# Attention and ternary feed-forward on one core: attention outputs stored without gaps, and Wo's product over two tiles of 128 rows

## The chip, the cores and the metric

The kernel runs on one core of a Trainium2 chip. The metric is the device time of one execution in microseconds (us), median of several runs.

## The reference

One transformer layer for a sequence of 4096 tokens of width 256, in f32:

```python
q, k, v = (x @ W.T + b, split into 16 heads of 16)      # Wq, Wk, Wv
q, k = rope(q), rope(k)
scores = softmax(q @ k.T / 16)                           # per head
x1 = layernorm(x + (scores @ v) @ Wo.T)
h = silu((x1 @ w1.T) * s1) * ((x1 @ w2.T) * s2)          # 256 -> 1024
h = gelu((h @ h1.T) * t1);  h = gelu((h @ h2.T) * t2)    # 1024 -> 1024, twice
out = layernorm(x1 + (h @ w3.T) * s3)                    # 1024 -> 256
```

The w and h matrices are ternary before a scaling of the inputs.

## The kernel before

The program has three parts, one after the other. Within a part every engine has its own instruction stream, and semaphores order them.

`project` computes q, k and v. `attend` works through 32 units: 8 chunks of 512 query tokens (CH), times 4 groups (NG) of 4 heads (HG). For one unit TensorE computes the scores of 128 keys by 512 queries, ScalarE takes their exponentials, and TensorE multiplies these with v (L547). The v tile has a 17th column of ones, so the products of one head fill 17 rows: 16 rows of output and one row of the softmax's sum. The four heads of a group lie at partitions 0, 32, 64 and 96 of the PSUM tile `sums`, so rows 17 to 31 of each stretch of 32 carry nothing of use. ScalarE copies this tile to `mixed` (L664, two buffers), and the queue of SyncE stores all 128 rows into `heads_dram` in one transfer (`finish`, L422 to L426). `attend` ends with SyncE waiting until the last stores have landed (L452 to L454).

`feed_forward` works through the 8 chunks of 512 tokens:

- `load_heads` (L847) loads one chunk as `heads_sb`, 128 partitions by 4 groups by 512, and then the chunk of x. For chunk c+2 it is issued once `front_apply` of chunk c+1 is done.
- `load_sums`, `store_inverse` and `load_shares` (L830 to L843): the sums' rows come in as 128 x 64, VectorE inverts them (`invert`, L1137), they go out to `shares_dram`, and are loaded again so that each head's row of 512 reciprocals is repeated over the head's partitions: four transfers of 64 KB for each of the four groups, into two buffers. VectorE multiplies them in (`divide`, L1148), one instruction for each group.
- `front` (L928) is Wo's product: per chunk 4 token tiles by 4 groups of 128 rows. The trace counts two matmuls for each f32 product, 32 per chunk. wo has the layout of heads_sb, with zeros in the rows without use; GpSimd sets them (L893).
- `gate_layer`, two `hidden_layer`s and `back` are the feed-forward products (L964, L1008). TensorE's order for chunk c, in `step`, is: hidden_layer 0, front(c+1), hidden_layer 1, front_flip(c+1) (L947), back(c), gate_layer(c+1).
- VectorE's `step` begins with divide(c+1, 0) and (c+1, 1), and places divides 2 and 3 behind the first two `gelu_split`s.

For chunk 0 the sums, stores and shares go through SyncE's queue, in this order: sums, heads, x, inverse, wo, scales, shares, then the large weights (L877). For later chunks GpSimd issues sums, inverse and shares, and SyncE issues the heads.

Of the kernel before, what the change touches and what calls it, by code (L numbers as in the profile page):

```python
# [328 lines left out]
def attend(nc, io, q_parts, k_parts, heads_dram, w_dram, low_bits, v_all, k_all):  # L329
# [6 lines left out]
    with ExitStack() as ctx:  # L336
# [72 lines left out]
        def _(sp):  # L409
# [42 lines left out]
            for p in range(2):  # L452
                sp.wait_ge(mixed_free[p], 16 + 16 * UNITS // 2)
            sp.wait_ge(w_copied, 16 * len(W_AT))  # L454
# [197 lines left out]
        @block.scalar  # L652
        def _(act):
            act.sem_inc(probs_free, RING // HG)

            act.wait_ge(first_turn, 1)
            act.activation(shift[:], scores[0][0:QT, 0:P], ACT.Copy, scale=-1.0).then_inc(exps_done, BANKS)

            def take_sums(c, g):

                act.wait_ge(probs_free, (c * NG + g + 1) * KT + RING // HG)

                act.wait_ge(mixed_free[g % 2], (c * 2 + g // 2) * 16 + 16)
                act.activation(mixed[g % 2][:], sums[:], ACT.Copy).then_inc(sums_free, 1)  # L664

            def unit(c, g, first=False, last=False):
                u = c * NG + g
                for n in range(TILES):
                    if n == TURN_AT and not last:
                        act.wait_ge(scored, u * SLOTS + n + 1)  # L670

                        act.wait_ge(part_step, (u + 2) * ROUNDS)
                        act.activation(shift[:], scores[n % BANKS][0:QT, 0:P], ACT.Copy, scale=-1.0)\  # L673
                            .then_inc(exps_done, 1)
                    s = slot(n, not last)
                    act.wait_ge(scored, u * SLOTS + s + 1)
                    if n % HG == 0:

                        act.wait_ge(probs_free, u * KT + n // HG + 1)
                    bank = last_banks[n % len(last_banks)] if last else scores[s % BANKS][:]  # L680
                    act.activation(probs[n % RING][:], bank, ACT.Exp, scale=INV_SCALE)\  # L681
                        .then_inc(exps_done, 1)
                    if n == HG - 1 and not first:
                        take_sums(*((c, g - 1) if g > 0 else (c - 1, NG - 1)))

            unit(0, 0, first=True)
            for c in range(NCH - 1):
                for g in range(1, NG):
                    unit(c, g)
                unit(c + 1, 0)  # L690
            for g in range(1, NG):
                unit(NCH - 1, g, last=g == NG - 1)
            take_sums(NCH - 1, NG - 1)

        @block.vector
        def _(dve):
# [25 lines left out]
            for p in range(2):  # L722
                dve.sem_inc(mixed_free[p], 16)
            dve.sem_inc(wide_free, 2)
# [13 lines left out]
def feed_forward(nc, io, heads_dram, shares_dram, w_dram, low_bits, out):  # L738
# [7 lines left out]
    with ExitStack() as ctx:  # L746
# [15 lines left out]
        flag = sb("flag", [1, 1], I32)  # L762
        heads = sb("heads_sb", [P, NG, CH])

        inverse_sums = sb("inverse_sums", [P, HG * NG * CH // P])
        shares = [sb(f"shares{b}", [P, CH]) for b in range(2)]
# [21 lines left out]
        x_in = sem("x_ff_in")  # L788
        wo_zero = sem("wo_zero")
        ident_set = sem("ident_ff_set")  # L790
# [27 lines left out]
        HIDS = 3 * HT  # L818
        SUM_COLS = HG * NG * CH // P
        SUM_ROWS = P // HG  # L820
        NORM1 = 4 * TT + 2
        NORM2 = 5 * TT + 2
        SMALL = HG + 4 + 1
        EARLY = 3
# [5 lines left out]
        def load_sums(engine, c, done):  # L830

            for j in range(HG):
                src = heads_dram[bass.ds(c, 1), 32 * j + HD].rearrange("c g (a b) -> (c g a) b", b=SUM_COLS)
                engine.dma_start(inverse_sums[j * SUM_ROWS:(j + 1) * SUM_ROWS], src).then_inc(done, 16)

        def store_inverse(engine, c, done):
            dst = shares_dram[bass.ds(c, 1)].rearrange("c j g (a b) -> (c j g a) b", b=SUM_COLS)
            engine.dma_start(dst, inverse_sums[:]).then_inc(done, 16)

        def load_shares(engine, c, g, done):  # L840
            for j in range(HG):
                src = shares_dram[bass.ds(c, 1), j, g].rearrange("c s -> (c s)").partition_broadcast(32)
                engine.dma_start(shares[g % 2][32 * j:32 * j + 32], src).then_inc(done[g % 2], 16)  # L843

        @block.sync
        def _(sp):
            def load_heads(c):  # L847
                sp.dma_start(heads[:], heads_dram[bass.ds(c, 1)].rearrange("c p g s -> (c p) g s")).then_inc(heads_in, 16)
                sp.dma_start(x_sb[:], io["x"].rearrange("(c t p) d -> c p t d", t=TT, p=P)[bass.ds(c, 1)]
# [20 lines left out]
            sp.wait_ge(first_inverse_out, 16)  # L870
            for g in range(NG):
                if g >= 2:

                    sp.wait_ge(divided, g - 1)
                load_shares(sp, 0, g, first_shares_in)

# [15 lines left out]
        def _(pool):  # L892
            pool.memset(wo[:], 0.0).then_inc(wo_zero, 1)  # L893
            pool.wait_ge(wo_zero, 1)
            pool.memset(ones[:], 1.0).then_inc(ident_set, 1)
# [8 lines left out]
            with pool.Fori(1, NCH) as c:  # L904
# [22 lines left out]
        def _(pe):  # L927
            def front(c):  # L928


                pe.wait_ge(divided, c * NG + NG)
                for t in range(TT):
                    if t % 2 == 0 and not (isinstance(c, int) and c == 0):

                        pe.wait_ge(norm2, (c - 1) * NORM2 + t + 2)
                    for g in range(NG):
# [173 lines left out]
        def _(dve):  # L1110
# [20 lines left out]
            def invert(c):  # L1131

                if isinstance(c, int) and c == 0:
                    dve.wait_ge(first_sums_in, HG * 16)
                else:
                    dve.wait_ge(sums_in, c * HG * 16)
                dve.reciprocal(inverse_sums[:], inverse_sums[:]).then_inc(inverted, 1)  # L1137

            def divide(c, g):

                if g == 0:
                    dve.wait_ge(heads_in, c * 16 + 16)

                if isinstance(c, int) and c == 0:
                    dve.wait_ge(first_shares_in[g % 2], (g // 2 + 1) * HG * 16)
                else:
                    dve.wait_ge(shares_in[g % 2], ((c - 1) * 2 + g // 2 + 1) * HG * 16)
                dve.tensor_tensor(heads[:, g], heads[:, g], shares[g % 2][:], ALU.mult).then_inc(divided, 1)  # L1148

# [85 lines left out]
            invert(0)  # L1235
            for g in range(NG):
                divide(0, g)
            dve.wait_ge(small_in, 16 * SMALL)
# [62 lines left out]
```

## Time and profile before

| | |
|---|---|
| time, median of 3 runs | 3553.01 us (3552.21 to 3554.25) |
| the profiled execution | 3551.05 us, of it 3549.4 us from its first to its last instruction (the span) |
| TensorE busy | 3414.3 us, 96% |
| VectorE busy | 2997.2 us, 84% |
| ScalarE busy | 2451.1 us, 69% |
| `attend` ends, `feed_forward` begins | at about 2785 us of the span |
| granted TensorE clock, mean | 0.971 |

A matmul's busy time overlaps that of its neighbours, so the duration of a stretch of them is read from the chain or from start to start.

### The profile page before, as it was taken

What the parts mean: (1) busy time and instruction counts of PE and PEld (TensorE: products, weight loads), DVE (VectorE), ACT (ScalarE), POOL (GpSimd) and SP (SyncE); (2) the same over time, 40 slices, a digit from 0 to 9 for tenths busy, and PEclk for the clock granted to TensorE, in tenths of its full rate; (3) what the DMA queues carried; (4) which work ended last, traced back from release to release, by engine and by line L of the source; (5) the groups of instructions that cost most, each with busy time, mean ns of one, the idle gap of its engine ahead of it and who ended that gap; (6) DMA issues with size and microseconds to landing.
All of it is one profiled execution on the core that took longest, in us unless ns stands there. A gap on an engine that the chain in (4) does not pass through costs nothing. (4 is left out here: it accounts for less than half of the span.)

```text
span 3549.4 us, 67886 instructions
## 1 busy us (share of the span) xinstructions
PE 3414.3 (96%) x28122; PEld 1560.8 (44%) x28122; DVE 2997.2 (84%) x3204; ACT 2451.1 (69%) x4472; POOL 242.7 (7%) x440
## 2 busy tenths in 40 slices
PE   8569999999999999999999999999999699999998
PEld 3223333333333333333333333333333388888887
DVE  6599999999999999999999999999994245555554
ACT  2108888888888888888888888888889422222222
POOL 3300000000000000000000000000000011111100
PEclk8759999999999999999999999999999799999999
DMA  8920000000000010001000000000000501111100
GB/s 211 222 36 12 16 14 14 25 13 13 14 30 18 12 62 13 14 13 61 18 17 25 15 14 14 14 14 13 17 8 5 187 31 37 37 37 37 37 19 13
DMA packets 64150, 126.12 MB, mean 36 GB/s; under 512 B 13447, under 2 KB 25800, under 8 KB 62648
## 3 DMA queue, kind: packets, MB, share of 16 engines
q1 hardware_dynamic: 54920, 102.49, 10.3%
q0 software_dynamic: 8928, 19.35, 1.9%
q8 instruction: 221, 3.62, 0.4%
q14 instruction: 81, 0.66, 0.1%
HBM read 90.59 MB, written 41.16 MB: 37 GB/s over the span
## 5 line engine op out<-in xcount | busy, mean ns | idle before, releaser
L710 DVE TENSOR_REDUCE group_max<-wide 128x2 f32<-128x1024 f32 x2048 | 2473.0, 1222 | 23.9 <-PE wide L521 17.2
L681 ACT ACTIVATE probs<-scores 128x512 f32<-128x512 f32 x4046 | 2202.9, 600 | 291.8 <-PE scores L606 43.9
L547 PE MATMUL sums<-probs,v_all 128*17 128x256 f32 (+1 forms) x16120 | 1277.9, 389 | 7.7 <-ACT mixed L664 6.8
L606 PE MATMUL scores<-q_sb,k_all 51*128 51x512 f32 x3968 | 989.0, 495 | 6.7 <-ACT probs L681 5.7
L521 PE MATMUL wide<-k_all,q_sb 48*128 48x512 f32 x4096 | 850.6, 411 | 52.4 <-DVE group_max L710 26.7
L606 PEld LDWEIGHTS scores<-q_sb,k_all 51*128 51x128 f32 x3968 | 370.9, 183 | 843.5 <-ACT probs L681 830.0
L547 PEld LDWEIGHTS sums<-probs,v_all 128*17 128x17 f32 x16120 | 267.1, 95 | 748.1 <-issue 365.8
L521 PEld LDWEIGHTS wide<-k_all,q_sb 48*128 48x128 f32 x4096 | 397.8, 191 | 91.0 <-DVE group_max L710 63.9
L1083 ACT ACTIVATE whole_hid<-acc,scale 128x512 f32<-128x512 f32 x128 | 84.7, 689 | 321.7 <-PE acc L964 316.9
L964 PE MATMUL acc<-hid_b,h2T 128*128 128x512 f32 x1024 | 241.6, 396 | 0.0
L964 PE MATMUL acc<-hid_a,h1T 128*128 128x512 f32 x1024 | 240.2, 394 | 0.0
L964 PEld LDWEIGHTS acc<-hid_b,h2T 128*128 128x128 f32 x1024 | 192.3, 188 | 46.4
L964 PEld LDWEIGHTS acc<-hid_a,h1T 128*128 128x128 f32 x1024 | 191.6, 187 | 47.3
L1173 DVE CAST hid_a<-whole_hid 128x512 fp32r<-128x512 f32 x128 | 54.4, 425 | 185.7 <-ACT whole_hid L1083 183.5
L1074 ACT ACTIVATE gate<-acc,scale 128x512 f32<-128x512 f32 x64 | 44.1, 690 | 125.9 <-PE acc L964 125.9
L229 PE MATMUL ps_qk<-xt,w_qk 128*128 128x512 f32 x128 | 72.6, 729 | 27.7 <-DMA xt<-in_xT 27.6
L1175 DVE TENSOR_TENSOR hid_a<-whole_hid,hid_a 128x512 fp32r<-128x512 f32 x128 | 88.6, 692 | 4.4
L1182 DVE SCALAR_TENSOR_TENSOR whole_hid<-acc,scale,gate 128x512 f32<-128x512 f32 x64 | 48.1, 751 | 44.9 <-PE acc L964 44.9
L937 PE MATMUL tok<-wo,heads_sb 128*128 128x256 f32 x256 | 59.3, 392 | 17.8 <-DVE heads_sb L1148 17.8
L964 PE MATMUL acc<-x1t,w1T 128*128 128x512 f32 x256 | 71.8, 402 | 2.1 <-DVE x1t L1167 2.1
L1173 DVE CAST hid_b<-whole_hid 128x512 fp32r<-128x512 f32 x64 | 27.1, 424 | 55.1 <-ACT whole_hid L1083 55.0
L483 POOL CAST shift_parts<-shift 16x128 bf16<-16x128 f32 x32 | 8.9, 279 | 932.7 <-ACT shift L673 896.7
(89 smaller groups left out, 1295.0 us busy)
## 6 DMA issues: line engine op xcount, KB each, us to landing
k_all<-k_parts SPq DMA_DIRECT2D x96, 128.0 KB, 5.1
q_sb<-q_parts SPq DMA_DIRECT2D x192, 64.0 KB, 2.8
q_parts<-parts SPq DMA_DIRECT2D x16, 512.0 KB, 5.9
k_parts<-parts SPq DMA_DIRECT2D x16, 512.0 KB, 6.3
heads<-mixed SPq DMA_DIRECT2D x32, 256.0 KB, 2.6
heads_sb<-heads SPq DMA_DIRECT2D x8, 1024.0 KB, 4.9
shares<-shares_dram POOLq DMA_DIRECT2D x112, 64.0 KB, 2.3
xt<-in_xT SPq DMA_DIRECT2D x8, 512.0 KB, 6.3
```

The lines of the kernel that those rows point to most:

```text
L229: last = pe.matmul(ps[m][:], w_sb[:, t, i, ft * P:(ft + 1) * P], xt[p][:, i], start=(i == 0), stop=(i == FT - 1))
L521: last = pe.matmul(wide[n % 2][:, e], q_sb[g][rows, j, t * P:(t + 1) * P], k_all[rows, g * GP + j, b * CH:(b + 1) * CH], start=True, stop= ...
L547: last = pe.matmul(sums[32 * j:32 * j + HD + 1, cols], v_all[:, g, kt, j], probs[(kt * HG + j) % RING][:, cols], start=(kt == 0 and cols.s ...
L606: pe.matmul(scores[(s + e) % BANKS][:], k_all[rows, g * GP + j, n // HG * P:(n // HG + 1) * P], q_sb[g][rows, j], start=True, stop=True).t ...
L681: act.activation(probs[n % RING][:], bank, ACT.Exp, scale=INV_SCALE)\
L710: dve.reduce_max(group_max[:, n], wide[n % 2][:], AX_X).then_inc(wide_free, 1)
L937: last = pe.matmul(tok[t // 2][:, t % 2], heads[:, g, t * P:(t + 1) * P], wo[:, g], start=(g == 0), stop=(g == NG - 1))
L964: mm = pe.matmul(dst, w.bitcast(view), src[h].bitcast(view), start=(first and h == 0), stop=(last and h == 1))
L1083: act.activation(whole[o % 4][:], acc[n % 4][:], ACT.Gelu, scale=scale[:, 2 + layer, o:o + 1])\
L1173: dve.tensor_copy(dst[0][:, k % HT], whole[k % 4][:]).then_inc(rounded, 1)
L1175: dve.tensor_tensor(dst[1][:, k % HT], whole[k % 4][:], dst[0][:, k % HT].bitcast(F32), ALU.subtract)\
L1182: dve.scalar_tensor_tensor(out=whole[o % 4][:], in0=acc[(2 * o + 1) % 4][:], scalar=scale[:, 1, o:o + 1], in1=gate[o % 2][:], op0=ALU.mult ...
```

## The change

Heads lie in DRAM as 16 heads by 17 rows, without gaps. `finish` stores four pieces of 17 rows in place of one of 128. `load_heads` loads the 16 output rows of eight heads as one tile of 128 rows, twice. The sums come in by one transfer in place of four. The shares of a chunk are spread by two transfers, whose source has the dimensions 8 heads, 16 repeats, 512, in place of sixteen. `divide` runs twice per chunk, and `front` has 4 token tiles by 2 tiles of 128 rows, 8 products (16 matmuls in the trace's count). wo loads in one transfer, and GpSimd's memset of it is gone. `mixed_free` counts four transfers for each store.

```diff
@@ attend
             def finish(c, g):
                 sp.wait_ge(sums_free, c * NG + g + 2)
-                sp.dma_start(heads_dram[bass.ds(c, 1), :, g].rearrange("c p s -> (c p) s"), mixed[g % 2][:])\
-                    .then_inc(mixed_free[g % 2], 16)
+                for j in range(HG):
+                    sp.dma_start(heads_dram[c, g * HG + j], mixed[g % 2][32 * j:32 * j + HD + 1]).then_inc(mixed_free[g % 2], 16)
@@ feed_forward
-        wo = sb("wo", [P, NG, D])
+        wo = sb("wo", [P, FT, D])
-        heads = sb("heads_sb", [P, NG, CH])
+        heads = sb("heads_sb", [P, FT, CH])
         def load_sums(engine, c, done):
-            for j in range(HG):
-                src = heads_dram[bass.ds(c, 1), 32 * j + HD].rearrange("c g (a b) -> (c g a) b", b=SUM_COLS)
-                engine.dma_start(inverse_sums[j * SUM_ROWS:(j + 1) * SUM_ROWS], src).then_inc(done, 16)
+            src = heads_dram[bass.ds(c, 1), :, HD].rearrange("c h (a b) -> (c h) a b", b=SUM_COLS)
+            engine.dma_start(inverse_sums[:], src).then_inc(done, 16)
-        def load_shares(engine, c, g, done):
-            for j in range(HG):
-                src = shares_dram[bass.ds(c, 1), j, g].rearrange("c s -> (c s)").partition_broadcast(32)
-                engine.dma_start(shares[g % 2][32 * j:32 * j + 32], src).then_inc(done[g % 2], 16)
+        def load_shares(engine, c, f, done):
+            src = shares_dram[bass.ds(c, 1), f * HF:(f + 1) * HF].rearrange("c h s -> (c h) s")
+            engine.dma_start(shares[f][:], src.unsqueeze(1).to_broadcast([HF, HD, CH]))\
+                .then_inc(done[f], 16)
             def load_heads(c):
-                sp.dma_start(heads[:], heads_dram[bass.ds(c, 1)].rearrange("c p g s -> (c p) g s")).then_inc(heads_in, 16)
+                for f in range(FT):
+                    src = heads_dram[bass.ds(c, 1), f * HF:(f + 1) * HF, 0:HD].rearrange("c h d s -> (c h) d s")
+                    sp.dma_start(heads[:, f], src).then_inc(heads_in, 16)
-            sp.wait_ge(wo_zero, 1)
-            for j in range(HG):
-                sp.dma_start(wo[32 * j:32 * j + HD], io["woT"].rearrange("(g j d) o -> j d g o", g=NG, j=HG)[j])\
-                    .then_inc(small_in, 16)
+            sp.dma_start(wo[:], io["woT"].rearrange("(f p) o -> p f o", p=P)).then_inc(small_in, 16)
@@ GpSimd
-            pool.memset(wo[:], 0.0).then_inc(wo_zero, 1)
-            pool.wait_ge(wo_zero, 1)
-                for g in range(NG):
-                    pool.wait_ge(divided, c * NG + g - 1)
-                    if g == 0:
-                        pool.wait_ge(inverse_out, c * 16)
-                    load_shares(pool, c, g, shares_in)
+                pool.wait_ge(inverse_out, c * 16)
+                for f in range(FT):
+                    pool.wait_ge(divided, (c - 1) * FT + f + 1)
+                    load_shares(pool, c, f, shares_in)
@@ TensorE, front
-                    for g in range(NG):
-                        last = pe.matmul(tok[t // 2][:, t % 2], heads[:, g, t * P:(t + 1) * P], wo[:, g],
-                                         start=(g == 0), stop=(g == NG - 1))
+                    for f in range(FT):
+                        last = pe.matmul(tok[t // 2][:, t % 2], heads[:, f, t * P:(t + 1) * P], wo[:, f],
+                                         start=(f == 0), stop=(f == FT - 1))
@@ VectorE, step
                 if not final:
-                    for g in range(2):
-                        divide(c + 1, g)
+                    divide(c + 1, 0)
                 for o in range(HT):
                     gelu_split(c, 0, o)
-                    if not final and o < 2:
-                        divide(c + 1, 2 + o)
+                    if not final and o == 0:
+                        divide(c + 1, 1)
@@ build
-    heads_dram = nc.dram_tensor("heads", [NCH, P, NG, CH], F32, kind="Internal").ap()
-    shares_dram = nc.dram_tensor("shares_dram", [NCH, HG, NG, CH], F32, kind="Internal").ap()
+    heads_dram = nc.dram_tensor("heads", [NCH, H, HD + 1, CH], F32, kind="Internal").ap()
+    shares_dram = nc.dram_tensor("shares_dram", [NCH, H, CH], F32, kind="Internal").ap()
```

## Rows read from the trace of the kernel before

**Rows 1.** Windows of one steady feed-forward chunk: busy us of engines, clock, DMA share, GB/s

```profile
2963.00:3053.00 90.00, 90.00 (x426) 74.42 (x425) 47.95 (x105) 22.95 (x32) 10.52 (x21) 1.00 0.11 36
```

**Rows 2.** Chain that ended last, from chunk 0's gate layer on: start, us, what

```profile
2825.06 47.81 PE acc L964 x192
2872.88 6.91 PE tok L937 x32
...
2918.07 44.80 PE acc L964 x192
2962.87 6.91 PE tok L937 x32
```

**Rows 3.** The same chain at the head of feed_forward

```profile
2785.38 0.35 SPq L834
...
2786.70 1.78 DMA inverse_sums<-heads
...
2789.08 5.61 DMA shares_dram<-inverse_sums
...
2802.36 1.98 DMA shares<-shares_dram
...
2804.36 0.70 DVE heads_sb L1148
...
2805.20 9.88 PE tok L937 x32
```

**Rows 4.** SyncE's queue at the end of attend and behind it, from the timeline

```profile
2782.55 0.34 SPq L425 DMA_DIRECT2D heads<-mixed  x1
2785.38 1.76 SPq L834 DMA_DIRECT2D inverse_sums<-heads  x4
2787.18 0.42 SPq L848 DMA_DIRECT2D heads_sb<-heads  x1
```

**Rows 5.** Windows, all engines' columns: the two transfers from 3 partitions (2 x 384 KB, L437), then the last heads store

```profile
190.00:192.00 2.00, 1.33 (x6) 0.55 (x4) 2.00 (x3) 0.00 (x0) 0.00 (x0) 0.50 0.18 23
...
210.00:218.00 8.00, 5.56 (x14) 2.01 (x14) 8.00 (x9) 0.00 (x0) 0.47 (x1) 0.50 0.12 26
...
2783.50:2784.00 0.50, 0.00 (x0) 0.00 (x0) 0.00 (x0) 0.00 (x0) 0.00 (x0) 0.50 1.01 385
```

**Rows 6.** DMA issues of feed_forward: KB each, median us to landing

```profile
heads_sb<-heads SPq DMA_DIRECT2D x8, 1024.0 KB, 4.9
shares<-shares_dram POOLq DMA_DIRECT2D x112, 64.0 KB, 2.3
...
heads<-mixed SPq DMA_DIRECT2D x1, 256.0 KB, 2.4
```

**Rows 7.** Windows around the two rises of TensorE's clock (third column from the right)

```profile
2810.00:2811.00 1.00, 1.00 (x4) 0.85 (x3) 0.00 (x0) 0.00 (x0) 0.00 (x0) 0.64 0.98 369
2831.00:2832.00 1.00, 1.00 (x5) 0.78 (x5) 0.15 (x1) 0.25 (x1) 0.00 (x0) 0.90 1.10 353
```

**Rows 8.** Timeline of GpSimd's and VectorE's part in the shares of chunk 3

```profile
3028.65 2.23 POOL L843 DMA_DIRECT2D shares<-shares_dram  x4 [1.90 <-DMA shares_dram<-inverse_sums]
...
3042.05 0.69 DVE L1148 TENSOR_TENSOR heads_sb<-heads_sb,shares 128x512 f32<-128x512 f32 x1 [2.17 <-DMA shares<-shares_dram]
```

**Rows 9.** Timeline where hidden_layer 0 ends and front follows

```profile
2962.97 0.69 ACT L1083 ACTIVATE whole_hid<-acc,scale 128x512 f32<-128x512 f32 x1 [3.05 <-PE acc L964]
2964.15 0.69 DVE L1175 TENSOR_TENSOR hid_b<-whole_hid,hid_b 128x512 fp32r<-128x512 f32 x1
```

**Rows 10.** Waits of SyncE's queue: us in total, times, longest

```profile
SPq L420 <- POOL shift_rows L494: 2064.2, 32, 80.0
```

**Rows 11.** Timeline of SyncE's queue: the large weights

```profile
2802.82 0.42 SPq L879 DMA_DIRECT2D w1T<-ff_weights  x1
...
2820.93 7.85 SPq L848 DMA_DIRECT2D heads_sb<-heads  x1
```

**Rows 12.** Window in which the large weights' transfers end

```profile
2837.00:2838.00 1.00, 1.00 (x6) 0.80 (x5) 1.00 (x2) 0.26 (x1) 0.00 (x0) 1.00 0.22 70
```

More of the change, by code:

```diff
@@ L452, in _ @@
             for p in range(2):
-                sp.wait_ge(mixed_free[p], 16 + 16 * UNITS // 2)
+                sp.wait_ge(mixed_free[p], 16 * HG * (1 + UNITS // 2))
             sp.wait_ge(w_copied, 16 * len(W_AT))
@@ L661, in take_sums @@
                 act.wait_ge(probs_free, (c * NG + g + 1) * KT + RING // HG)
-                act.wait_ge(mixed_free[g % 2], (c * 2 + g // 2) * 16 + 16)
+                act.wait_ge(mixed_free[g % 2], (c * 2 + g // 2 + 1) * 16 * HG)
                 act.activation(mixed[g % 2][:], sums[:], ACT.Copy).then_inc(sums_free, 1)
@@ L722, in _ @@
             for p in range(2):
-                dve.sem_inc(mixed_free[p], 16)
+                dve.sem_inc(mixed_free[p], 16 * HG)
             dve.sem_inc(wide_free, 2)
@@ L762, in feed_forward @@
         flag = sb("flag", [1, 1], I32)
-        heads = sb("heads_sb", [P, NG, CH])
-        inverse_sums = sb("inverse_sums", [P, HG * NG * CH // P])
+        heads = sb("heads_sb", [P, FT, CH])
+        inverse_sums = sb("inverse_sums", [P, H * CH // P])
         shares = [sb(f"shares{b}", [P, CH]) for b in range(2)]
@@ L788, in feed_forward @@
         x_in = sem("x_ff_in")
-        wo_zero = sem("wo_zero")
         ident_set = sem("ident_ff_set")
@@ L818, in feed_forward @@
         HIDS = 3 * HT
-        SUM_COLS = HG * NG * CH // P
-        SUM_ROWS = P // HG
+        SUM_COLS = H * CH // P
+        HF = H // FT
         NORM1 = 4 * TT + 2
         NORM2 = 5 * TT + 2
-        SMALL = HG + 4 + 1
+        SMALL = 1 + 4 + 1
         EARLY = 3
@@ L830, in load_sums @@
         def load_sums(engine, c, done):
[L832 to L834 removed]
+            src = heads_dram[bass.ds(c, 1), :, HD].rearrange("c h (a b) -> (c h) a b", b=SUM_COLS)
+            engine.dma_start(inverse_sums[:], src).then_inc(done, 16)
         def store_inverse(engine, c, done):
[L837 removed]
+            dst = shares_dram[bass.ds(c, 1)].rearrange("c h (a b) -> (c h a) b", b=SUM_COLS)
             engine.dma_start(dst, inverse_sums[:]).then_inc(done, 16)
[L840 to L843 removed]
+        def load_shares(engine, c, f, done):
+            src = shares_dram[bass.ds(c, 1), f * HF:(f + 1) * HF].rearrange("c h s -> (c h) s")
+            engine.dma_start(shares[f][:], src.unsqueeze(1).to_broadcast([HF, HD, CH]))\
+                .then_inc(done[f], 16)
         @block.sync
@@ L870, in _ @@
             sp.wait_ge(first_inverse_out, 16)
-            for g in range(NG):
-                if g >= 2:
-                    sp.wait_ge(divided, g - 1)
-                load_shares(sp, 0, g, first_shares_in)
+            for f in range(FT):
+                load_shares(sp, 0, f, first_shares_in)
             for name, (at, rows, cols) in W_AT.items():
@@ L928, in front @@
             def front(c):
-                pe.wait_ge(divided, c * NG + NG)
+                pe.wait_ge(divided, c * FT + FT)
                 for t in range(TT):
@@ L935, in front @@
                         pe.wait_ge(norm2, (c - 1) * NORM2 + t + 2)
-                    for g in range(NG):
-                        last = pe.matmul(tok[t // 2][:, t % 2], heads[:, g, t * P:(t + 1) * P], wo[:, g],
-                                         start=(g == 0), stop=(g == NG - 1))
+                    for f in range(FT):
+                        last = pe.matmul(tok[t // 2][:, t % 2], heads[:, f, t * P:(t + 1) * P], wo[:, f],
+                                         start=(f == 0), stop=(f == FT - 1))
                     if t % 2 == 1:
@@ L1133, in invert, with divide @@
                 if isinstance(c, int) and c == 0:
-                    dve.wait_ge(first_sums_in, HG * 16)
+                    dve.wait_ge(first_sums_in, 16)
                 else:
-                    dve.wait_ge(sums_in, c * HG * 16)
+                    dve.wait_ge(sums_in, c * 16)
                 dve.reciprocal(inverse_sums[:], inverse_sums[:]).then_inc(inverted, 1)
[L1139 to L1148, printed above, removed]
+            def divide(c, f):
+                if f == 0:
+                    dve.wait_ge(heads_in, (c + 1) * FT * 16)
+                dve.wait_ge(first_shares_in[f] if c == 0 else shares_in[f], 16 if c == 0 else c * 16)
+                dve.tensor_tensor(heads[:, f], heads[:, f], shares[f][:], ALU.mult).then_inc(divided, 1)
             def front_stats(c, p):
@@ L1235, in _ @@
             invert(0)
-            for g in range(NG):
-                divide(0, g)
+            for f in range(FT):
+                divide(0, f)
             dve.wait_ge(small_in, 16 * SMALL)
```

## The prediction

> **What bounds the kernel now.** I read the page first, for the shares of the engines, then the chain of work that ended last, then windows of one chunk, then the timeline at the seam between attend and feed_forward. The page says that TensorE is busy for 96% of the span, which leaves open where it is the bound. The chain answers that for the part the change touches. From chunk 0's gate layer to the last back product it is TensorE without a break, in a pattern that repeats seven times, and Wo's product stands in it with 6.91 us for 32 matmuls [rows 2]. The windows agree: in the 90 us of one chunk TensorE is busy for all 90, at full clock, while VectorE has 48 us of work and ScalarE 23 [rows 1]. So in these chunks a matmul removed is time removed, as long as nobody else comes late. Ahead of the first product the chain is a series of small transfers with TensorE idle: sums, inverse, shares, divide [rows 3]. There the issue times and the landings count, not the bytes alone.
>
> **Wo's product in the seven later fronts.** 32 matmuls take 6.91 us, 0.216 us each, with full rows of 256 columns before and after. 16 of them go: 3.45 us. Times 7: **-24.2 us**. What was beside them? The last gelu of hidden_layer 0 and its split by VectorE run from 2962.97 to 2964.84 [rows 9], some 2.0 us behind the end of that layer at 2962.87 [rows 2]. The front that remains is 3.45 us long and still covers them; besides, hidden_layer 1 needs that tile last, behind three times 14 matmuls (`EARLY`). No stall is put in. The statistics and the flip that follow front wait on other work than front's end, and keep their distance to hidden_layer 1.
>
> **The first front.** It took 9.88 us, since TensorE had been idle and worked at the lower clock (1.2 GHz) until about 2810.6, 5.4 us in [rows 3, 7]. At half the clock one of these matmuls takes 2 x 0.216 = 0.43 us. 5.4 us are 12.6 matmuls, the other 3.4 at full clock 0.73: 6.1 us. If the clock rises later than all 16 it is 6.9, if a little earlier 5.2. I take **-3.8 us** (bounds -3.0 and -4.7). The next rise is 6 us behind the gate layer's start; the stretch of 192 matmuls with it is 47.81 against 44.80 without, so it costs 3.0 us today [rows 2, 7]. After a shorter front this may be 1.5 more or less; I put 0.
>
> **The sums.** Of four issues the last starts 1.32 us behind the first, and its transfer takes 1.78 [rows 3]. One issue remains, so **-1.3 us**. The heads' load, whose issue stands behind them, moves forward as much, at least [rows 4].
>
> **The last heads store.** Here a term of the other sign comes in. Before, one store of 256 KB lands 2.4 us after its issue [rows 4, 6], with the DMA engines full at 385 GB/s, 24 GB/s for each of 16 [rows 5]. The new stores have 17 rows each. No transfer of the trace has that form. The nearest that isn't a multiple of 16 is the pair from 3 partitions: it kept the DMA engines busy at 0.18, three of sixteen (0.1875), at 23 to 26 GB/s, and towards its end at 0.12, two of them [rows 5]. So a transfer there was cut evenly by its rows, and a prime number like 17, more than the 16 engines, can't be cut evenly except onto one. On that reading all four pieces go over one engine: 68 rows of 2 KB. A row takes 2048 B / 24 GB/s = 0.085 us, so 5.8 us of data; it starts 0.7 us behind the issue, as before, and lands 0.85 behind its end: 7.35 in place of 2.4, **+5.0 us** with nothing beside it. If instead the rows spread over all engines, only three further issues of 0.37 are added, +1.1. The dearest case is one engine at the pace of the 3-partition pair: 24 GB/s over 3 engines is 0.25 us for a row, 17 us, +16. I take +5.0, since the store itself ran at 0.085 and only the width is in question.
>
> The Trainium skill has a rule for the width ("DMA: Bandwidth & Descriptors", the section on why a DMA increments its semaphore by 16): the number of engines is the largest up to 16 that divides the slowest dimension of both sides. By it 17 rows go to one engine, and a source whose outer dimension is 8 goes to eight. The 3-row pair agrees with it (0.18 of the DMA). With the rule the term is the +5.0 above; without it +1.1.
>
> In attend's other 31 units the store is not on the path: the queue waits 2064 us in all for the next shift rows [rows 10], and a buffer of mixed is needed again two units later, some 160 us. Three issues of 0.37 us and 5 us of landing disappear there. If that cover were gone it would be 1.1 us for each unit.
>
> **Heads and inverse.** Both heads loads together are 512 KB in place of 1024. With a source whose outer dimension is 8, an even cut puts them on 8 engines: 64 KB for each of these, as 1024 KB on 16 before. Behind them the x load is unchanged. So the engines that are fullest have as much as before, and the inverse, which queues behind, lands 5.6 us after its issue still: **0**. If they go over all 16 it is 32 KB less for each, at 24 GB/s -1.35 us.
>
> **The shares of chunk 0.** From the inverse's landing at 2794.69 to the first matmul at 2805.20 there are 10.5 us: sixteen issues, a buffer wait in the middle, the landing, the divide of 0.70 and 0.14 [rows 3]. After, two issues: the second at +0.4, its data starting at +0.8. On 8 engines the two carry 64 KB each, 2.7 us, until +3.5, with 1.1 to land, 0.7 to divide and 0.14 for the wait: 5.45. **-5.05 us**. On 16 engines it would be 4.1 (-6.4). At 3-partition pace, 32 rows x 0.25 = 8 us, it is 10.8: +0.2, no gain. The wo and scale transfers ahead of them are issued 1.3 us faster (one in place of four) and don't bind. GpSimd's memset of wo (0.95 us) was beside the sums and is worth 0.
>
> **Later chunks: sums, shares, divides.** GpSimd issues 3 transfers in place of 20 and VectorE saves two divides, all beside TensorE: 0. Today the shares are issued at 3028.65, the last divide ends at 3042.74 [rows 8] and front starts at 3052.9 (2962.87 + 90.0) [rows 1, 2]. Divide 1 stands behind one split now and needs no buffer; it is earlier, not later. The new wait (both heads loads) comes long before: they are issued when front_apply of the chunk before is done, most of a chunk ahead, and take 5 us [rows 6].
>
> **The weights.** They are issued right behind the shares, about 7 us sooner relative to the inverse's landing; the gate layer starts 9 us sooner relative to it (5.05 + 3.8). Today they are issued from 2802.8 and their tail ends at about 2837 [rows 11, 12], while the gate layer's 64 matmuls (64 x 44.80 / 192 = 15, and 3 for the clock, from 2825.06) end near 2843 [rows 2]: 2 us less of a margin of 6. No stall.
>
> **Sum.** -24.2 - 3.8 - 1.3 + 5.0 + 0 - 5.05 = -29.4 us. The profiled execution took 3551.05 us for a span of 3549.4; that becomes 3521.7 for 3520.0. The median of the runs is 2.0 us above the profiled execution, so I add it: **3523.6 us**.
>
> **The rivals.**
> A. Everything spreads over 16 engines. The full DMA share for 128-row loads speaks for it, the 0.18 of the 3-row pair against it. Store +1.1, heads -1.35, shares -6.4: 3553.0 - 24.2 - 3.8 - 1.3 + 1.1 - 1.35 - 6.4 = 3517.1 us. Chance 0.2.
> B. Narrow transfers, and slow for each row as the 3-partition pair was. That pair reads and writes SBUF and repeats a source row, as the shares do from DRAM. Store +16, shares +0.2: -24.2 - 3.8 - 1.3 + 16 + 0.2 = -13.1, 3539.9 us; half of it (the store at its own pace, only the shares slow) gives 3528.8. Chance 0.16 for both.
> C. The other side: the shares' transfers of the later chunks go over one engine at 0.25 us for a row. 128 rows are 32 us, two are 64. Issued 24.2 us before front, they would hold TensorE for about 40 us in each of 7 chunks: 3553 + 7 x 40 less the gains, some 3810 us. It turns slower than before once the stall exceeds 29.4 / 7 = 4.2 us, that is once the second lands 28 us or more after its issue; 64 KB take 2.3 today [rows 6], and the rows' outer dimension of 8 speaks against one engine. Chance 0.03.
> D. The product isn't halved in time, because other work in the chunk binds at once. VectorE's 48 of 90 us speak against it [rows 1]; the last split ends 2 us behind layer 0, front is 3.45. If half were lost, +12: 3535.7 us. Chance 0.04.
>
> **Chances and range.** The forecast has 0.55, A 0.2, B 0.16, C 0.03, D 0.04, and 0.02 remain for an effect in attend that no row shows. The likeliest case alone reaches from 3520 to 3527 (clock phase 1.5, first front 1, run offset 1). The range takes in A and the milder half of B, and stops at 3532; about 0.15 lie outside. The measurement can tell 0.2%, 7 us, from no change; all cases but C and the remainder are below that: faster 0.95, same 0.01, slower 0.04.
>
> **What the profile would show.** Front in the steady chunks: x16, about 3.45 us, chunk to chunk 86.55 us in place of 90.0, TensorE without gaps. The first front: about 6 us. The last heads store: landing near 7 us and a DMA share near 0.06 while it runs (rival A: 2 to 3 us and a high share). Store of the inverse to the first matmul: 5.4 us. The prediction is wrong if TensorE waits for heads_sb or hid_b in the steady chunks, if attend's span before 2782 moves, or if the seam takes longer than today.

## The result and the profile after

The changed kernel takes 3524.65 us (median of 4 runs, 3524.46 to 3526.26) against 3552.61 for the kernel before in the same comparison: an estimated ratio of 0.9927, 95% interval 0.9915 to 0.9939, clear of 1 (the two medians by themselves give 0.9921). The forecast was 3523.6 us. The profiled execution has a span of 3523.1 us against 3549.4, 26.3 us less.

The chain that ended last, of the changed kernel: the head of feed_forward and the first chunk (start, us, what).

```profile
2790.86 2.67 DMA inverse_sums<-heads
...
2794.14 4.84 DMA shares_dram<-inverse_sums
2798.98 0.02 issue
2799.00 0.63 SPq L840
2799.63 0.04 issue
2799.67 5.68 DMA shares<-shares_dram
2805.35 0.02 issue
2805.37 0.71 DVE heads_sb L1134
2806.08 0.14 issue
2806.21 6.43 PE tok L927 x16
...
2822.63 47.85 PE acc L954 x192
2870.47 3.45 PE tok L927 x16
...
2912.21 44.80 PE acc L954 x192
2957.01 3.45 PE tok L927 x16
```

From one Wo product to the next it is 2957.01 - 2870.47 = 86.54 us, against 89.99 in [rows 2]; the product itself is 3.45 us for 16 matmuls. The window of that chunk, with the columns of [rows 1], shows TensorE without a gap, as before:

```profile
2870.47:2957.01 86.54, 86.54 (x410) 71.37 (x409) 46.65 (x103) 22.93 (x31) 2.46 (x4) 1.00 0.08 26
```

The other half of the story is SyncE's queue at the seam, from its timeline. It answers to [rows 4]:

```profile
2782.39 1.25 SPq L426 DMA_DIRECT2D heads<-mixed  x4
2790.86 0.66 SPq L832 DMA_DIRECT2D inverse_sums<-heads  x1
2791.57 1.30 SPq L848 DMA_DIRECT2D heads_sb<-heads  x2
```

From the last store's issue to the first issue of feed_forward it was 2.83 us (2782.55 to 2785.38); now it is 8.47. And three windows of the changed kernel inside that stretch, with DMA share and GB/s last:

```profile
2783.00:2784.00 1.00, 0.00 (x0) 0.00 (x0) 0.00 (x0) 0.00 (x0) 0.00 (x0) 1.00 0.06 12
...
2787.00:2788.00 1.00, 0.00 (x0) 0.00 (x0) 0.00 (x0) 0.00 (x0) 0.00 (x0) 0.50 0.07 25
...
2789.00:2790.00 1.00, 0.00 (x0) 0.00 (x0) 0.00 (x0) 0.00 (x0) 0.00 (x0) 0.50 0.07 27
```

A sixteenth is 0.0625. Where [rows 5] show 1.01 and 385 GB/s for the old store, the four new ones keep about one engine busy, at 12 to 27 GB/s. The trace's single DMA packets say the same without an average: from 2783.11 to 2790.06 there are 68 of 2 KB, each starting as the one before it ends. And each of the four transfers has a single landing in the trace's semaphore events (increments made at the issue, before any data moved, left out), where the one store of the padded kernel below has sixteen.

The difference of 26.3 us, piece by piece (before minus after, from the two chains):

| piece | predicted | measured |
|---|---|---|
| seven later fronts | -24.2 | -24.2 (7 x (6.91 - 3.45)) |
| first front | -3.8 | -3.45 (9.88 to 6.43) |
| sums, first issue to landing | -1.3 | -0.4 (3.1 to 2.67) |
| seam, last store to first issue | +5.0 | +5.6 (2.83 to 8.47) |
| inverse's landing | 0 | -0.8 (5.61 to 4.84) |
| inverse's landing to first matmul | -5.05 | -3.3 (10.5 to 7.23) |
| the rest (end of attend, first gate layer, tail) | 0 | +0.2 |
| sum | -29.4 | -26.3 |

### The profile page after: what moved, and what is told of

Same layout as the page of the kernel before. It is cut to its first block and busy times, and to the rows that moved or that the text cites. A ratio compares the mean times of both kernels' runs of the same rounds, so it can differ in the third digit from the quotient of the medians.

```text
span 3523.1 us, 67331 instructions
## 1 busy us (share of the span) xinstructions
PE 3384.9 (96%) x27994; PEld 1536.3 (44%) x27994; DVE 2987.0 (85%) x3188; ACT 2451.1 (70%) x4472; POOL 184.7 (5%) x320
## 5 line engine op out<-in xcount | busy, mean ns | idle before, releaser
L229 PE MATMUL ps_qk<-xt,w_qk 128*128 128x512 f32 x128 | 72.4, 729 | 28.8 <-DMA xt<-in_xT 28.8
L954 PE MATMUL acc<-x1t,w2T 128*128 128x512 f32 x256 | 71.3, 400 | 0.0
```

The lines of the kernel that those rows point to most:

```text
L229: last = pe.matmul(ps[m][:], w_sb[:, t, i, ft * P:(ft + 1) * P], xt[p][:, i], start=(i == 0), stop=(i == FT - 1))
L954: mm = pe.matmul(dst, w.bitcast(view), src[h].bitcast(view), start=(first and h == 0), stop=(last and h == 1))
```

## The experiments

Each is the changed kernel with the edit shown. Times of different comparisons are set against the kernel before, timed in the same comparison. Kernels that ran only once, for their profile, are judged by pieces of the chain. Their single times (3521.44 us with 16-row pieces, 3553.55 with the products done twice, 3529.02 and 3521.42 with the wide source, 3528.68 with the weights held, 3526.85 with the sums in four) differ by more than the effects, for a reason told at the end.

**One store of 128 rows, heads padded to 32 rows in DRAM.**

```diff
-                for j in range(HG):
-                    sp.dma_start(heads_dram[c, g * HG + j], mixed[g % 2][32 * j:32 * j + HD + 1]).then_inc(mixed_free[g % 2], 16)
+                sp.dma_start(heads_dram[c, g * HG:(g + 1) * HG].rearrange("h p s -> (h p) s"), mixed[g % 2][:])\
+                    .then_inc(mixed_free[g % 2], 16)
-    heads_dram = nc.dram_tensor("heads", [NCH, H, HD + 1, CH], ...)
+    heads_dram = nc.dram_tensor("heads", [NCH, H, 2 * HD, CH], ...)
```

> The changed kernel, but with heads in DRAM as 16 heads by 32 rows, so that one store of 128 rows (256 KB) takes the place of the four of 17; loads and products as changed. Theory: the 5.6 us by which the seam (last copy to mixed until SyncE's first issue in feed_forward) grew, 2.8 to 8.44, come from four 17-row stores on one DMA engine. Then the seam is 2.8 again, the store's DMA share near 1 for under 1 us, and the time is 5.6 us under the changed kernel: about 3519. Rival, the growth comes from four issues and four completions and not from the width: also gone here, so this run alone sizes the cost, and the run with 16-row pieces tells the two apart. Second rival, the new loads of heads are what gained or lost: the rest of the opening (15.4 us from the first issue to the first matmul) moves by over 1 us; I expect it within 0.5.

Measured: 3518.25 us, before 3550.08 in that comparison; ratio 0.9915, interval 0.9899 to 0.9932. Its timeline of SyncE's queue:

```profile
2779.72 0.34 SPq L425 DMA_DIRECT2D heads<-mixed  x1
2782.20 0.68 SPq L832 DMA_DIRECT2D inverse_sums<-heads  x1
```

The seam is 2.48 us, 6.0 less than in the changed kernel and 0.35 less than before the change. The rest of the opening, first issue to first matmul, was 16.66 us (2782.20 to 2798.86) against 15.35, outside the 0.5 I allowed. Of this, +2.2 are the inverse's landing (7.04 us). It isn't the layout's doing: it was 5.42 in a second profile of the same kernel, and 5.0 to 5.7 in six other runs.

**The same question with 16-row pieces.**

```diff
                 for j in range(HG):
-                    sp.dma_start(heads_dram[c, g * HG + j], mixed[g % 2][32 * j:32 * j + HD + 1]).then_inc(mixed_free[g % 2], 16)
+                    sp.dma_start(heads_dram[c, g * HG + j, 0:HD], mixed[g % 2][32 * j:32 * j + HD]).then_inc(mixed_free[g % 2], 16)
+                for j in range(HG):
+                    sp.dma_start(heads_dram[c, g * HG + j, HD:HD + 1].rearrange("o (a b) -> (o a) b", b=CH // 16),
+                                 mixed[g % 2][32 * j + HD:32 * j + HD + 1].rearrange("o (a b) -> o a b", b=CH // 16)).then_inc(mixed_free[g % 2], 16)
```

> The changed kernel with each head's store cut in two: 16 rows of output, and the one row of the sum as 16 pieces. Eight issues in place of four. Theory (a prime number of rows goes to one engine): the 16-row stores spread over the engines, so the seam is 2.8 plus 7 further issues of about 0.4, 5 to 6.2 us, against 8.44, and the DMA share peaks well above the 0.07 of the 17-row stores. Rival (many small stores are slow in themselves): the seam grows above 8.44, towards 11.

Timeline of SyncE's queue, then two windows of the stretch, of this kernel:

```profile
2782.45 1.71 SPq L426 DMA_DIRECT2D heads<-mixed  x4
2784.20 1.16 SPq L428 DMA_DIRECT2D heads<-mixed  x4
2786.72 0.67 SPq L835 DMA_DIRECT2D inverse_sums<-heads  x1
```

```profile
2783.00:2784.00 1.00, 0.00 (x0) 0.00 (x0) 0.00 (x0) 0.00 (x0) 0.00 (x0) 1.00 0.29 62
2784.00:2785.00 1.00, 0.00 (x0) 0.00 (x0) 0.00 (x0) 0.00 (x0) 0.00 (x0) 0.72 0.31 72
```

Twice as many issues for the same bytes, and the seam is 4.27 us, not 8.47: better than the 5 to 6.2 I expected, since the first stores run while the others are issued. The DMA share is 0.3 in place of 0.07. In the trace each 16-row transfer has sixteen landings, and each transfer of a sum's row has one: it went as one packet of 2 KB and not as 16 pieces, which does no harm with a single row. One row fewer in a piece halves the seam. The number of transfers isn't the cost; the 17 rows are.

**Wo's products done twice.**

```diff
-                    for f in range(FT):
-                        last = pe.matmul(tok[t // 2][:, t % 2], heads[:, f, t * P:(t + 1) * P], wo[:, f],
-                                         start=(f == 0), stop=(f == FT - 1))
+                    for n in range(2 * FT):
+                        last = pe.matmul(tok[t // 2][:, t % 2], heads[:, n % FT, t * P:(t + 1) * P], wo[:, n % FT],
+                                         start=(n == 0), stop=(n == 2 * FT - 1))
```

> The changed kernel with each of Wo's products done twice (32 matmuls per chunk as before, the attention output doubled ahead of the residual). Theory: the seven later fronts gained 24.2 us and the first 3.45, and nothing but the number of matmuls made that: front 6.91 us again, chunk 90.0 us, first front near 10, so the span is 27.6 +- 1.5 above the changed kernel's 3523.1, 3550.7. Rival, part of the gain came from fewer divides or transfers beside TensorE: the chunks stay under 90.0 us or the span under 3548.

Its span is 3551.9 us, its chain:

```profile
2875.09 6.91 PE tok L927 x32
...
2965.08 6.91 PE tok L927 x32
```

89.99 us per chunk again, with two divides per chunk in place of four and half the bytes of the heads and shares loads still gone. The gain in the chunks is the matmuls and nothing else. The first front took 8.89 us, one less than I expected; the span is 28.8 above the changed kernel's, of which 1.4 is an end of attend that came later and 1.3 a slower opening, so without these 26.1.

**The shares' source 16 rows wide.** First with other heads' reciprocals, then with each head's own, for which the inverse is stored twice.

```diff
-            src = shares_dram[bass.ds(c, 1), f * HF:(f + 1) * HF].rearrange("c h s -> (c h) s")
-            engine.dma_start(shares[f][:], src.unsqueeze(1).to_broadcast([HF, HD, CH]))\
+            src = shares_dram[bass.ds(c, 1)].rearrange("c h s -> (c h) s")
+            engine.dma_start(shares[f][:], src.unsqueeze(1).to_broadcast([H, HF, CH]))\
```

> The changed kernel, with the shares' source as 16 rows repeated 8 times (outer dimension 16) in place of 8 rows repeated 16 times; both transfers read the same reciprocals, which are not those of the heads they are multiplied into, so the sums' division is changed. Bytes, rows and issues are the same. Theory: the two transfers run on 8 DMA engines, and that is why inverse's landing to first matmul took 7.2 us. On 16 it should be 5.9 or less (16 rows less for each of the engines, at 0.085 to 0.14 us a row, 1.3 to 2.3 us less), the DMA share between the first data and the weights' data near 1 in place of 0.6. Rival: the rows are slow because a DRAM row is read again and again, or because the large weights come in beside them, and the width is nothing: 7.2 +- 0.3.

```diff
-            dst = shares_dram[bass.ds(c, 1)].rearrange("c h (a b) -> (c h a) b", b=SUM_COLS)
-            engine.dma_start(dst, inverse_sums[:]).then_inc(done, 16)
+            for e in range(2):
+                dst = shares_dram[bass.ds(c, 1), :, e].rearrange("c h (a b) -> (c h) a b", b=SUM_COLS)
+                engine.dma_start(dst, inverse_sums[:]).then_inc(done, 16)
-            engine.dma_start(shares[f][:], src.unsqueeze(1).to_broadcast([HF, HD, CH]))\
+            engine.dma_start(shares[f][:], src.unsqueeze(1).to_broadcast([2 * HF, HD // 2, CH]))\
```

> The changed kernel with the inverse stored twice and the shares read with an outer dimension of 16, all values right, weights as changed. Theory (width): inverse's landing to first matmul 5.9 us, as in the run with the wide source and other heads' reciprocals (5.97), against 6.6 to 8.4 with 8 engines; the inverse's second store costs 0.4 us. Rival (the 5.97 was chance): 6.6 or more.

From the inverse's landing to the first matmul: 5.97 and 5.91 us. Seven profiles with the 8-wide source and the weights behind it gave 7.23, 6.55, 8.37, 7.55, 6.06, 8.25 and 8.82, mean 7.5. The two lie under all seven, but one such number scatters by over 2 us. The trace's landings settle the number of engines: in chunk 0 each of the two transfers has eight, in all eight profiles with the 8-wide source, and sixteen in all four with the 16-wide one. The later chunks show the time, with 14 transfers each; the issues of feed_forward in the changed kernel and in the one with the inverse stored twice (KB each, median us to landing):

```profile
shares<-shares_dram POOLq DMA_DIRECT2D x14, 256.0 KB, 3.9
```

```profile
shares<-shares_dram POOLq DMA_DIRECT2D x14, 256.0 KB, 3.3
```

With 8 rows the median is 3.8 to 4.2 in eight profiles, with 16 rows 3.3 or 3.4 in four. The DMA share while chunk 0's shares run was 0.78 to 0.95 with the wide source (three half microseconds from 2807.0 on) and 0.51 to 0.65 in the changed kernel (from 2801.0 on), near the 1 and the 0.6 of the theory.

**The weights held until chunk 0 is divided.**

```diff
                 load_shares(sp, 0, f, first_shares_in)
+            sp.wait_ge(divided, FT)
             for name, (at, rows, cols) in W_AT.items():
```

> The changed kernel with the five large weight loads held until chunk 0's second divide is done. From the inverse's landing to the first matmul the changed kernel takes 7.2 us (6.6 to 8.4 over three other runs with the same transfers), against 5.45 predicted. Theory 1 (the weights' transfers, issued 0.04 us behind the shares, share the engines with them and push the second landing back): 5.4 to 5.9 us. Theory 2 (it is the width of 8 engines and their rows at 0.14 us): 7.2 +- 0.5, weights or not. With both true, about 6.3. The gate layer must not wait for weights: they are 6 us later and had some 6 us of margin, so up to 1 us may come back there.

6.46 us (2804.15 to 2810.61), between the two theories' numbers and inside the scatter of the seven. By itself this run settles nothing; held and 16 rows wide together, below (there with padded heads besides), gave 5.37 and 5.19, against 5.97 and 5.91 wide alone. So part of the delay is the weights' transfers: some 0.7 us with the wide source, and 1.1 with the 8-wide one if its single run is taken at its word.

With nothing beside the shares, this run also shows when their data begin. They were issued at 2804.16:

```profile
2805.00:2805.50 0.50, 0.00 (x0) 0.00 (x0) 0.00 (x0) 0.00 (x0) 0.45 (x1) 0.50 0.00 0
2805.50:2806.00 0.50, 0.00 (x0) 0.00 (x0) 0.00 (x0) 0.00 (x0) 0.00 (x0) 0.50 0.47 135
```

The first packet starts at 2805.56, 1.4 us behind the issue, and 1.4 it is with the wide source too (2800.11 after 2798.73 and 2798.34 after 2796.96).

The gate layer didn't wait for weights, but the layer behind it did. Its chain, and the issue of w3T in the timeline of SyncE's queue:

```profile
2842.66 0.70 DVE hid_a L1162
2843.37 0.84 issue
2844.20 30.10 PE acc L955 x128
```

```profile
2814.97 9.89 SPq L874 DMA_DIRECT2D w3T<-ff_weights  x1
```

hidden_layer 0 of chunk 0 is entered only when h1T, h2T and w3T have all landed, and w3T landed 29.0 us behind its issue, at 2844.0. TensorE stood for 0.96 us. In the changed kernel w3T landed at 2835.9 and the layer began at 2840.44, so 4.6 us of margin were there; holding the weights used them up.

**The sums in four transfers again.**

```diff
-            src = heads_dram[bass.ds(c, 1), :, HD].rearrange("c h (a b) -> (c h) a b", b=SUM_COLS)
-            engine.dma_start(inverse_sums[:], src).then_inc(done, 16)
+            for j in range(HG):
+                src = heads_dram[bass.ds(c, 1), j * NG:(j + 1) * NG, HD].rearrange("c h (a b) -> (c h) a b", b=SUM_COLS)
+                engine.dma_start(inverse_sums[32 * j:32 * j + 32], src).then_inc(done, 16)
```

> The changed kernel with the sums loaded by four transfers of 32 rows again, as before, from the layout without gaps. The prediction had -1.3 us for the one transfer in place of four; measured was 3.1 to 2.7 us from first issue to landing, -0.4. Theory: one transfer of 128 short rows (256 B) is itself about 0.9 us slower to land than 32 of them, 2.5 to 2.7 in five runs against 1.78; with four it is 3.1 again from the first issue (last landing 1.8 behind the last issue). Rival: the 2.7 comes from the layout (rows 17 x 2 KB apart) or from the heads' loads issued right behind: then the last landing is 2.5 or more behind the last issue, 3.8 in all.

The head of its chain:

```profile
2792.53 0.73 SPq L833
2793.26 0.05 issue
2793.31 0.66 SPq L833
2793.97 0.05 issue
2794.02 0.63 SPq L833
2794.65 0.04 issue
2794.69 2.04 DMA inverse_sums<-heads
```

4.2 us from the first issue, which neither side had. The last landing is 2.04 behind its issue, near the theory's 1.8; what neither saw is the issue: 0.63 to 0.73 us each where [rows 3] have 0.35 and the old queue's four issues took 1.76 together [rows 4]. The source's rows now lie in two dimensions (head, piece of 64) that can't be merged into one. The single transfer's issue is 0.66 too. So with this layout one transfer saves 1.5 us against four, but against the old layout only 0.4.

The count of dimensions alone doesn't make an issue long: wo's source in the changed kernel (128 rows, 2 tiles, 256) has three as well and is issued in 0.44 us. The transfers of the changed kernel that took 0.63 to 0.66 each (sums, heads, shares) have the tile's partitions spread over two dimensions on the DRAM side, and the doubled store of the inverse, 0.64 in place of 0.37, is of that kind too; those that took 0.37 to 0.49 (the inverse, x, wo, w1T, w2T, h1T) have one dimension for them. This was read from the queue's rows and not tried by itself.

**All together, and a repeat side by side.** Padded heads, inverse stored twice, weights held:

> The changed kernel with three changes together: heads padded to 32 rows in DRAM, one store of 128 rows; the inverse stored twice, so that the shares' source has an outer dimension of 16; the large weights held until chunk 0 is divided. Theory: the seam is 2.5 to 2.9 us (-5.6 to -6), the inverse's second copy costs one issue, +0.4, inverse's landing to first matmul is 5 us (-2.2). Together -7.5 us against the changed kernel: about 3517 where the changed kernel is at 3524.7, ratio to before 0.990. Rival (in the padded run the inverse landed 7.0 us after its issue against 4.8 to 5.7 elsewhere: the padded layout loads slower): the inverse lands 7 us after its issue here too, and the gain is 5.5 us or less.

3518.5 us, before 3551.14; ratio 0.9907 (0.9891 to 0.9924). That is above the 3517 I expected; how far it is under the changed kernel, the next table says. The inverse's second copy landed 5.3 us after the first one's issue, so the padded layout isn't slow. Then the changed kernel, the padded one and this one, measured together:

> The changed kernel itself, timed beside the padded one and the one with all three changes on one chip. Over the profiles so far the seam is 8.4 to 8.5 us in every run with 17-row stores, while the end of attend moves by 8 us from one execution to another with the moment at which TensorE's clock rises in its first unit. Expected 27 to 29 us under the kernel before. Rival (the prediction's sum with the seam right and the shares off was luck): over 31 or under 25.

> The padded layout with one store of 128 rows, again. Theory (the seam, 6.0 us): 5 to 7 us under the changed kernel's median of the same call. Rival (the earlier 3518 was lucky in attend's clock, since its profiled run ended attend 2.7 us early): 3 us or less.

> Padded layout, inverse stored twice with a 16-wide source for the shares, weights held. Theory: 1.5 to 2 us under the padded kernel (inverse's landing to first matmul 5.4 against about 7.1 on average, 0.6 lost on the second store's issue), which the scatter of attend, some us, may hide. Rival: no gain over the padded one, or slower since the weights come later (the gate layer then waits for h1T).

| kernel | median us | range | ratio to before (95%) |
|---|---|---|---|
| before | 3550.49 | 3548.77 to 3553.79 | |
| changed | 3525.32 | 3523.45 to 3531.49 | 0.9929 (0.9915 to 0.9942) |
| padded | 3519.14 | 3517.13 to 3520.05 | 0.9910 (0.9895 to 0.9925) |
| all together | 3518.77 | 3516.33 to 3519.89 | 0.9909 (0.9893 to 0.9924) |

The changed kernel is 25.2 us under the kernel before here, where I had written 27 to 29 and given the rival under 25: neither, though the intervals of the two measurements of it (0.9929 and 0.9927) are nearly the same. The padded one is 6.2 under the changed one, the 6.0 of the seam. All together is 6.6 under the changed one, where I had expected 7.5 and its rival said 5.5 or less. Its last step, from padded to all together, is 0.4, not told apart from nothing, where I had expected 1.5 to 2. In its profile the opening, first issue to first matmul, is 3.7 us shorter than in the padded one's (13.6 against 17.3), but the padded profile's 8.82 from landing to matmul is the long end of the scatter.

Two pieces of the profiles say more than the medians here. From the last heads store's issue to the end of the span it is 766.9 us before, 740.7 and 741.6 in the two profiles of the changed kernel, 734.8 and 735.6 padded, 732.1 and 732.0 all together: the last step is some 3 us there, of which 1.7 in the first padded profile is its late inverse. Both profiles of all together had attend end late (last store at 2787.6 and 2786.1, against 2779.7 and 2782.6), which hides it in their spans; why the medians don't show it isn't settled. Second, the hold adds nothing to the wide source: from the inverse's landing to chunk 1's Wo product it is 68.87 and 69.15 us with the wide source alone, 68.91 and 68.80 with the weights held as well. hidden_layer 0 starts 0.2 us behind w3T's landing in both of these (2837.52 after 2837.32, 2835.63 after 2835.43), with 0.3 to 0.4 us idle ahead of it.

## Why the prediction was right, and where it was off

- **Seven fronts, -24.2.** Exact, and shown to be the matmuls alone by doing them twice: the chunk is 89.99 us again. Rival D is out: TensorE has no gap in the 86.54 us.
- **The last heads store, +5.0.** The mechanism was right and the size nearly: +5.6. The DMA share of 0.06 to 0.07, and the 68 packets one behind the other, say one engine. By the Trainium skill's rule ("DMA: Bandwidth & Descriptors", the section on why a DMA increments its semaphore by 16), 17 rows go to one engine and 16 to sixteen; the trace agrees on both, with one landing for each 17-row transfer and sixteen for each 16-row one. Rival A, with +1.1 here, is refuted. The term that was small is the data's time: 68 rows from 2783.11 to 2790.06, 6.95 us and not 5.8. The 0.085 us a row taken from the store over 16 engines was right (the median packet took 0.084), but 9 of the 68 took longer, up to 0.47 us, all in the first 4 us, which ran at 12 to 20 GB/s and not at 25 to 27. All seven profiles with these stores have the same stretch, 6.90 to 6.95 us; what makes those packets long isn't shown. The last landing is 8.0 us behind the first issue, where I had 7.35. Rival B's 0.25 of the 3-partition pair is far off.
- **In attend the narrow stores cost nothing.** The first heads store in the timeline of SyncE's queue, before and changed:

```profile
351.83 0.38 SPq L425 DMA_DIRECT2D heads<-mixed  x1
```

```profile
351.68 1.34 SPq L426 DMA_DIRECT2D heads<-mixed  x4
```

From here to the last one it is 2430.72 us before (to 2782.55) and 2430.71 changed (to 2782.39), across 31 units.
- **The shares of chunk 0, -5.05.** Too large: -3.3 in the first profile, -3.0 in the mean of the seven. The 8 engines were as predicted; what ran on them was mis-sized. The issue of such a transfer is 0.63 us, not 0.4, and the data began 1.4 us behind the first issue, not 0.8. With nothing beside them the data then took 3.8 us (2805.56 to 2809.36) and not 2.7, and landed 0.4 behind their end and not 1.1: 6.46 in place of 5.45. And the weights, which I had put right behind them at no cost, made it 6.06 to 8.82. I had the weights' move in the working only as a question for the gate layer; that they share engines with the shares was missing. A source 16 wide would have been worth about 1.6 us here (7.5 against 5.9), holding the weights 0.7 to 1.1, of which w3T's later landing takes back some or all.
- **The sums, -1.3.** Measured -0.4. I took the landing of an 8 KB transfer with a flat source for one of 32 KB with 128 short pieces: 2.46 to 2.70 us in place of 1.78, 0.3 of it the longer issue. The remaining 0.6 comes with the size of the transfer and not with the distance of its pieces in DRAM: from the end of its issue one transfer of 32 pieces lands in 1.4 us in the old layout (1.78 less 0.41) and in the new one (2.04 less 0.63), the one of 128 pieces in 2.0 (2.67 less 0.66). Whether the 128 pieces or the 32 KB do it was not separated.
- **The inverse's landing, 0.** It was -0.8 in the profile, but 4.8 to 7.0 over the runs, around the 5.6 of before. The 0 was fair, and this -0.8 is chance.
- **The first front, -3.8.** -3.45. The clock rose at the same distance from the first matmul as before, 5.5 us (0.62 in the window from 2811 to 2812, 0.64 in [rows 7]); it is the pace ahead of the rise that was mis-sized. I took twice 0.216, 0.43 us a matmul, 12.6 of them. The old front itself says less: 9.88 us with 4.4 at full clock leave 11.8 matmuls for the first 5.5 us, 0.47 each, and with that the new front comes to 6.4 us, as measured (6.43). Over the other profiles with 16 matmuls the rise came 3.1 to 5.9 us behind the first one and the front took 5.2 to 6.6 us, so the -3.45 belongs to this pair. The second rise cost the same 3.0 as before.
- **Rival C** (shares so late that VectorE holds TensorE) would have needed 28 us; the later chunks' transfers land in 3.9.

The four mis-sized terms (shares, sums, seam, first front) all erred to the same side, 3.6 us together; the lucky inverse took 0.8 back, the rest added 0.2, and the span came out 3.1 us above the 3520.0 forecast. The median is only 1.0 above its forecast, since the 2.0 that I added from profiled execution to median was absent this time: that is the scatter of single executions, not insight.

One of the prediction's own signs of being wrong also came up: the seam took longer. From the last store's issue to the first matmul it is 22.65 us before (2782.55 to 2805.20) and 23.82 now (2782.39 to 2806.21), 1.2 more, where the prediction's terms for it add up to 1.35 less. The whole gain is TensorE's shorter fronts; the seam, with its cheaper shares and dearer store, lost a little.

## What to carry to other kernels

A product that stands on a gap-free TensorE chain paid back its matmuls to the tenth of a microsecond here, whatever else the change moved. Choose the layout that makes this possible by the outer dimension of every transfer on the way: 17 rows ran on one DMA engine and cost 6 us where nothing covered them, while a padding that stores 1.9 times the bytes was free. Read the seams between stages for such transfers, since in the steady part they hide.

## What the runs showed that was not expected

Over thirteen profiles of kernels whose attend stage is the same but for the stores, its end moves by 8.5 us. It follows the moment at which TensorE's clock rises from 1.2 to 2.4 GHz in attend's first unit. Two windows each of the padded kernel and of the changed kernel's repeat (granted clock third from the right), and the last copy to mixed of the repeat:

```profile
272.00:274.00 2.00, 2.00 (x16) 0.45 (x12) 1.23 (x1) 1.08 (x2) 0.00 (x0) 0.69 0.00 0
274.00:276.00 2.00, 2.00 (x24) 0.66 (x22) 1.75 (x2) 1.86 (x4) 0.00 (x0) 1.00 0.00 0
```

```profile
284.00:286.00 2.00, 2.00 (x16) 0.65 (x12) 1.09 (x2) 0.99 (x2) 0.00 (x0) 0.50 0.00 0
286.00:288.00 2.00, 2.00 (x20) 0.73 (x16) 1.66 (x2) 1.19 (x4) 0.00 (x0) 0.98 0.00 0
```

```profile
2787.65 0.60 ACT L664 ACTIVATE mixed<-sums 128x512 f32<-128x512 f32 x1 [1.17 <-PE sums L547]
```

In the padded kernel's profile the clock rises near 273 us and the last copy ends at 2779.7; in the repeat of the changed kernel it rises near 286 and the copy ends at 2788.3. Until about 270 us TensorE, at the low level, waited for VectorE in short pauses (23 us of them from 190 to 268 us in both); from then on it was busy without a break and still at the low level, for some 5 us in the padded run and 16 in the repeat. Over the thirteen the order holds nearly throughout: the rise moves from 273.3 to 286.2 us, the last store's issue from 2779.7 to 2788.3. So two single profiles of this kernel may differ by 8 us with no cause in the code, and pieces have to be compared, or medians, not spans. Most of the movement lies ahead of the first heads store, which is issued between 349.0 and 356.3 us; from there to the last one it is 2430.7 to 2431.8 us with padded heads and 2430.7 to 2432.6 with 17-row stores. Why the clock rises when it does was not tried. Beside that the seam was constant: 8.4 to 8.5 us in each of the six further profiles with the 17-row stores, 2.5 in the four with the padded one.
